# A recommendation tower on one core: the linear layer's output turned to features on partitions, its root taken one step later

## The chip, the cores and the metric

One Trainium2 chip, one of its cores. The metric is the device time of the whole program in microseconds (us), median of the runs shown. Times inside the program come from one profiled execution.

## What is computed

For 512 samples, 26 embedding rows of 64 numbers each are fetched by index, passed through a linear layer and two layer norms, mixed from 26 to 32 rows, and joined with one row made of the dense features. All pairwise inner products of the 33 rows of a sample go through a linear layer (528 to 512) with a layer norm, of which 384 outputs are used, and then through three top layers. Cut to what matters (float32 throughout):

```python
e = stack([tbl_f[ids[:, f]] for f in range(26)], axis=1)      # 512 x 26 x 64
x = layer_norm(dense_t @ Wd.T, gd, bd)                        # 512 x 128
y = layer_norm(einsum('bnd,ed->bne', e, Ws), gs, bs)          # 512 x 26 x 128
y = layer_norm(einsum('bne,pn->bep', y, Wsi), gsi, bsi)       # 512 x 128 x 32
T = concatenate([x[:, None, :], swapaxes(y, 1, 2)], axis=1)   # 512 x 33 x 128
Z = einsum('bnd,bmd->bnm', T, T)                              # 512 x 33 x 33
z = layer_norm(Z[:, TRIL_I, TRIL_J] @ Wl.T, gl, bl)[:, :384]
h = concatenate([z, dense_t], axis=1)
h = maximum(h @ W_top1 + b_top1, 0)                           # 512 wide
h = maximum(h @ W_top2 + b_top2, 0)                           # 256 wide
y = h @ W_top3                                                # 512 x 1
```

## The kernel before

The 512 samples are 4 blocks of 128; a block is 4 units of 32 samples, so there are 16 units and 16 steps `t` (0 to 15), and step `t` works mainly on unit `t`. All engines are programmed by hand, each with its own `step(t)`, and meet only through semaphores; within an engine the order of the text is the order of the work.

- GpSimd (POOL) does one thing for most of the run: 104 indirect gathers (line 239), two for each of the 52 slots of 128 embedding rows. A block has 13 slots; its four units need 4, 3, 3 and 3 new ones. Nothing holds the gathers back.
- In step `t` TensorE (PE) runs `mix(t)` (line 281), which waits for the gathered rows of unit `t` to be scaled (`scale_a`, line 712), then `transposes(t+1)` (line 255), which waits for the gathers of unit `t+1`, then `project(t)` (line 293), `norms(t+1)` (line 266) and `inner(t-1)` (line 305), the inner products of the unit before.
- ScalarE (ACT) runs `keep_u(t)` (line 528), which brings the mixed rows from PSUM and is what `project(t)` waits for, `rows_out(t+1)` (line 515), two `squares_b` (line 534), small roots (`deviation_a`, `deviation_b`), and four `keep_z(t-1, 0..3)` (line 562), which bring the inner products from PSUM and write them across samples into `Zs`.
- VectorE (DVE) runs `add_b` twice (line 719), `mult_a`, `sums_a`, `recip_a` and `scale_a` for unit `t+1`, and `sums_b`, `recip_b` and `norm_b` (line 737) for unit `t`.
- When a block's products are kept, seven small transfers (`relay`, line 196) lay them out on partitions in `Zt`. For the last block the first half goes two units early; the second half is sent after the last product is kept, split over the queues of SP (three), ACT (two) and POOL (two).
- The linear layer and the top layers of block `b` run inside later steps, by `b, j = (t - 6) // 4, (t - 6) % 4`. In step j = 0 PE does the first two of five products of `linear` (line 323), in j = 1 the other three and `layer2` of block b-1, in j = 2 `turn` and a quarter of `layer1`, in j = 3 the rest of `layer1` and `output(b-1)`.
- In `linear` samples are on partitions and the 512 features are the moving side (5 matmuls of 512 columns). So the layer norm works along a row: `stat_w` and `norm_w` on VectorE with one root on ScalarE (a number per partition). The normed values are then turned by PE (`turn`, line 335) and copied back by ScalarE (`keep_zT`, line 574), for which `layer1` (line 347) waits. `layer1` starts from a matmul that puts the dense part `hd` into PSUM (line 340), and `relu1` adds the bias in four instructions (line 583).
- After step 15 the tail runs `inner(15)`, `turn` and `layer1` of block 2, then `last_block`: the dense part, `linear(3)` on all of its transfers, `layer2(2)`, three turns, `layer1` feature by feature, `layer2`, `output`, and a last copy (line 777).

```python
mm = pe.matmul(psW[:, :], Zt[0:KL, b, jj, :], wl_g[0:KL, jj, :], start=(jj == 0),
               stop=(jj == CW - 1))
```

## Time and profile before

| what | value |
|---|---|
| median of 3 runs | 186.33 us (184.78 to 186.76) |
| the profiled execution, whole | 185.44 us |
| its span, first to last instruction | 183.6 us |
| busy PE / DVE / ACT / POOL | 143.7 / 127.4 / 99.6 / 105.7 us |
| mean granted clock of TensorE | 0.972 |

The span lies 1.84 us below the execution's own time. Times in the rows are us from the start of the span. Engines work side by side, so busy times don't add up; a float32 matmul shows as two records in the trace, so that "x10" below is five matmuls.

### The profile page before, as it was taken

What the parts mean: (1) busy time and instruction counts of PE and PEld (TensorE: products, weight loads), DVE (VectorE), ACT (ScalarE), POOL (GpSimd) and SP (SyncE); (2) the same over time, 40 slices, a digit from 0 to 9 for tenths busy, and PEclk for the clock granted to TensorE, in tenths of its full rate; (3) what the DMA queues carried; (4) which work ended last, traced back from release to release, by engine and by line L of the source; (5) the groups of instructions that cost most, each with busy time, mean ns of one, the idle gap of its engine ahead of it and who ended that gap; (6) DMA issues with size and microseconds to landing.
All of it is one profiled execution on the core that took longest, in us unless ns stands there. A gap on an engine that the chain in (4) does not pass through costs nothing.

```text
span 183.6 us, 4383 instructions
## 1 busy us (share of the span) xinstructions
PE 143.7 (78%) x1693; PEld 96.5 (53%) x1693; DVE 127.4 (69%) x297; ACT 99.6 (54%) x233; POOL 105.7 (58%) x111
## 2 busy tenths in 40 slices
PE   0089877899984854899984989699859998869995
PEld 0084444525954433466652675467447654646583
DVE  6099659695989588486989497686957797730321
ACT  3003335582867585556858387755675885812130
POOL 0778777777778778778777777777773000040000
PEclk9999999999998799659999999999999999999999
DMA  4912716141111113111111221111113001020000
GB/s 135 290 49 31 300 22 199 29 118 46 34 27 26 25 25 89 38 29 28 27 26 24 66 65 26 29 31 22 28 40 77 0 5 32 12 34 3 0 0 0
DMA packets 6891, 9.58 MB, mean 52 GB/s; under 512 B 3923, under 2 KB 4056, under 8 KB 6743
## 3 DMA queue, kind: packets, MB, share of 16 engines
q0 software_dynamic: 3504, 3.46, 10.1%
q1 hardware_dynamic: 2845, 5.08, 8.5%
q10 hardware_dynamic: 522, 0.77, 1.7%
q8 instruction: 13, 0.21, 0.4%
q14 instruction: 7, 0.06, 0.1%
HBM read 8.01 MB, written 0.00 MB: 44 GB/s over the span
## 4 chain that ended last, share of the span: by engine, by line
POOL 46%; PE 24%; issue 17%; ACT 5%; DVE 4%; DMA 4%; ACTq 0%; DVEq 0%
POOL g_sb L239 46%; PE psW L323 5%; PE psW L347 3%; PE psH L361 3%; PE psB L293 2%; DMA ids_sb<-in_ids 2%; PE psU L281 2%; PE psZ L305 2%; ACT Zs L562 2%; DMA g_sb<-in_table,row_id 1%; DVE B L719 1%; PE psG L266 1%; ACT U L528 1%; PE psB L388 1%; DVE qA L697 1%
## 5 line engine op out<-in xcount | busy, mean ns | idle before, releaser
L239 POOL DMA_INDIRECT g_sb<-in_table,row_id x104 | 103.1, 991 | 31.7 <-issue 31.4
L562 ACT ACTIVATE Zs<-psZ 32x264 f32<-32x264 f32 x62 | 38.0, 613 | 1.1
L719 DVE TENSOR_TENSOR B<-psB,bias 128x512 f32<-128x512 f32 x32 | 20.6, 685 | 24.2 <-PE psB L293 24.2
L534 ACT ACTIVATE sqB<-B 128x512 f32<-128x512 f32 x32 | 19.7, 632 | 22.0 <-DVE B L719 20.5
L281 PE MATMUL psU<-wsi_x,g_sb 128*128 128x192 f32 (+4 forms) x128 | 22.0, 316 | 10.4 <-DVE g_sb L712 8.0
L281 PEld LDWEIGHTS psU<-wsi_x,g_sb 128*128 128x128 f32 x128 | 19.7, 194 | 16.3 <-DVE g_sb L712 12.6
L737 DVE TENSOR_TENSOR T<-B,rB 128x512 f32<-128x512 f32 x32 | 22.2, 693 | 1.1
L293 PE MATMUL psB<-U,ws_g 64*128 64x512 f32 x64 | 19.6, 692 | 3.7 <-ACT U L528 3.7
L726 DVE TENSOR_REDUCE ssB<-sqB 128x16 f32<-128x512 f32 x32 | 21.6, 678 | 0.1
L266 PEld LDWEIGHTS psG<-gram,sT 128*128 128x128 f32 x104 | 13.4, 198 | 13.4 <-ACT sT L515 10.8
L323 PE MATMUL psW<-wl_g,Zt 127*128 127x512 f32 x40 | 19.5, 621 | 0.4 <-ACT h1T L583 0.4
L266 PE MATMUL psG<-gram,sT 128*128 128x128 f32 x104 | 16.6, 300 | 0.7 <-ACT sT L515 0.7
L255 PE MATMUL psT<-small_sb,g_sb 128*128 128x128 f32 x52 | 11.4, 299 | 4.6 <-DMA g_sb<-in_table,row_id 4.3
L196 POOL DMA_DIRECT2D Zt<-Zs x2 | 2.3, 1137 | 21.9 <-DVE Zs L906 21.9
L528 ACT ACTIVATE U<-psU 128x512 f32<-128x512 f32 x16 | 9.5, 596 | 9.1 <-PE psU L281 8.9
L305 PE MATMUL psZ<-T 128*32 128x33 f32 x1024 | 14.2, 201 | 0.0
L305 PEld LDWEIGHTS psZ<-T 128*32 128x32 f32 x1024 | 12.0, 112 | 3.1 <-issue 1.0
L347 PE MATMUL psW<-zT,w_g 128*128 128x128 f32 x72 | 9.4, 282 | 5.4 <-ACT zT L574 5.4
L347 PEld LDWEIGHTS psW<-zT,w_g 128*128 128x128 f32 x72 | 8.4, 191 | 7.9 <-ACT zT L574 7.8
L323 PEld LDWEIGHTS psW<-wl_g,Zt 127*128 127x128 f32 x40 | 7.2, 195 | 7.3 <-issue 7.1
L515 ACT ACTIVATE sT<-psT 128x384 f32<-128x384 f32 (+1 forms) x16 | 8.2, 515 | 4.7 <-PE psT L255 4.7
L255 PEld LDWEIGHTS psT<-small_sb,g_sb 128*128 128x128 f32 x52 | 6.9, 153 | 7.3 <-DMA g_sb<-in_table,row_id 7.3
(128 smaller groups left out, 184.8 us busy)
## 6 DMA issues: line engine op xcount, KB each, us to landing
g_sb<-in_table,row_id POOLq DMA_INDIRECT x104, 2.5
wl_sb<-in_wl SPq DMA_DIRECT2D x1, 1280.0 KB, 5.5
w_sb<-in_w SPq DMA_DIRECT2D x2, 512.0 KB, 5.7
w_sb<-in_w SPq DMA_DIRECT2D x1, 768.0 KB, 4.3
small_sb<-in_small SPq DMA_DIRECT2D x1, 615.5 KB, 7.0
dense_sb<-in_dense ACTq DMA_DIRECT2D x1, 512.0 KB, 3.7
Zt<-Zs SPq DMA_DIRECT2D x3, 80.0 KB
Zt<-Zs SPq DMA_DIRECT2D x3, 70.0 KB
```

The source lines that it names most:

```text
L239: pool.indirect_dma_start(g_sb[:, k, h * DSP:(h + 1) * DSP], None, table, bass.IndirectOffsetOnAxis(row_id[:, 2 * k + h:2 * k + h + 1], 0) ...
L266: mm = pe.matmul(psG[:, n * P:(n + 1) * P], sT[:, u % 2, n * P:(n + 1) * P], gram[:, :], start=True, stop=True)
L281: mm = pe.matmul(psU[:, (lo - US * j) * PROJ:(hi - US * j) * PROJ], g_sb[:, SLOTS * b + c, :], wsi_x[:, c, lo - s0:hi - s0, :], start=(n = ...
L293: pe.matmul(psB[h][:, :], ws_g[h * DSP:(h + 1) * DSP, :], U[h * DSP:(h + 1) * DSP, u % 2, :], start=True, stop=True).then_inc(B_done, 1)
L305: mm = pe.matmul(psZ[gq * PROJ:(gq + 1) * PROJ, n * COLS:(n + 1) * COLS], T[:, u % 2, h, s, 2:2 + PROJ], T[:, u % 2, h, s, 0:COLS], start= ...
L323: mm = pe.matmul(psW[:, :], Zt[0:KL, b, jj, :], wl_g[0:KL, jj, :], start=(jj == 0), stop=(jj == CW - 1))
L347: mm = pe.matmul(psW[:, f * BS:(f + 1) * BS], w1_g[:, k, f * P:(f + 1) * P], zT[:, k * BS:(k + 1) * BS], start=False, stop=(k == KZ - 1), ...
L534: act.activation(sqB[:, h, :], B[:, h, :], ACT.Square).then_inc(B_squared, 1)
L562: act.activation(to, product, ACT.Copy).then_inc(Z_kept, 1)
L719: dve.tensor_tensor(B[:, h, :].rearrange("p (s j) -> p s j", j=PROJ), psB[h][:, :].rearrange("p (s j) -> p s j", j=PROJ), bias[:, :].rearr ...
L726: dve.tensor_reduce(ssB[:, h, :], sqB[:, h, :].rearrange("p (s j) -> p s j", j=PROJ), AX, ALU.add).then_inc(B_summed, 1)
L737: dve.tensor_tensor(T[:, u % 2, h, :, 2:], B[:, h, :].rearrange("p (s j) -> p s j", j=PROJ), rB[:, h, :].rearrange("p (s o) -> p s o", o=1 ...
```

## The change

The linear layer changes sides. The weights are now stationary in pieces of 128 features and the samples are the moving side: 20 matmuls of 128 columns instead of 5 of 512, with the 512 features of a block's 128 samples on partitions. 12 of the 20 run in step j = 0, the other 8 in j = 1, now ahead of `inner`. `Zs` and `Zt` hold the samples in two halves of 64.

The mean of the layer norm is taken off the weights beforehand: VectorE sums `wl` over features (t = 1) and subtracts it where it scales the weights (now t = 2), and the shift of the extra rows gets its mean off too (t = 2, and an activation in ScalarE's step 3, formerly step 2). The variance is made by squaring the 512 features on ScalarE (`squares_w`) and summing over partitions with a matrix of ones on PE (`variance`, four matmuls of 128 columns), both in j = 1. The root (`deviation_w`, now 128x128) stands at the head of ScalarE's j = 2, the reciprocal (`recip_w`, now 128x128) at the head of VectorE's. The un-normed features go straight from PSUM to `zT` (VectorE, end of j = 1), `layer1` uses them without a turn, whole in j = 2, and its result is scaled by the reciprocal and added to the dense part by VectorE at the head of j = 3 (`scale_h1`, `add_hd`, 128x512 each), then `relu1` is one instruction. `turn`, `keep_zT` on ScalarE, `stat_w`, `norm_w` and the matmul with `hd` are gone. `layer2(b)` runs in j = 3; `relu2`, `output` and `copy_y` of block b come at the head of the next j = 0. The bias is added to `hd` once, in four activations in ScalarE's steps 4 to 7; scaling `w1` moves from VectorE to ScalarE (three activations, t = 2).

In the tail the last unit's products go to another PSUM bank, so `inner(15)` waits for no eviction; `variance(2)` and `layer1(2)` follow; the last block's linear layer is put out in two PSUM banks; `layer2(2)` stands after `layer1(3)`, and `output(2)` just ahead of the last output.

The diff, cut to its core (eight columns of indentation removed):

```diff
+Zs = sb("Zs", [PROJ, 2, 2, 7 * CW, PS])
+Zt = sb("Zt", [P, BLOCKS, 2, CW, PS])
+zT = sb("zT", [P, KZ * BS])
+z_sq = sb("z_sq", [P, FLIN // P * BS])
...
+zr = sb("zr", [P, BS])
...
+psL, psV, psF, psO = [psZ, psT], psU, psB, [psG, psT]
+psS = [psH, psH, psG]
...
+    b, lo = u // BU, 2 * US * (u % 2) + GQ * gq
+    bank = psZ if u < UNITS - 1 else psU
+    return (Zs[:, b % 2, u % BU // 2, 0:COLS, lo:lo + GQ].rearrange("p c s -> p s c"),
+            bank[gq * PROJ:(gq + 1) * PROJ, 0:GQ * COLS].rearrange("p (s c) -> p s c", s=GQ))
...
+    queue.dma_start(Zt[BASE[q]:BASE[q] + ROWS[q], b, lo:hi, :, :],
+                    Zs[FIRST[q] - 1:PROJ, b % 2, lo:hi, CW * q:CW * (q + 1), :]).then_inc(landed, 16)
...
+        if u == UNITS - 1:
+            pe.wait_ge(U_ready, UNITS)
+        elif u:
             pe.wait_ge(Z_kept, 4 * u)
+        bank = psZ if u < UNITS - 1 else psU
...
-                    mm = pe.matmul(psZ[gq * PROJ:(gq + 1) * PROJ, n * COLS:(n + 1) * COLS],
+                    mm = pe.matmul(bank[gq * PROJ:(gq + 1) * PROJ, n * COLS:(n + 1) * COLS],
...
+            pe.wait_ge(d_zt[b], 7 * 16)
+            if b:
+                pe.wait_ge(y_copied, b)
...
-        for jj in range(lo, hi):
-            mm = pe.matmul(psW[:, :], Zt[0:KL, b, jj, :], wl_g[0:KL, jj, :], start=(jj == 0),
-                           stop=(jj == CW - 1))
-        if hi == CW:
+        for n in range(lo, hi):
+            f, jj = n // CW, n % CW
+            mm = pe.matmul(psW[:, f * BS:(f + 1) * BS], wl_g[0:KL, jj, f * P:(f + 1) * P],
+                           Zt[0:KL, b, :, jj, :], start=(jj == 0), stop=(jj == CW - 1))
...
+    def variance(b):
+        pe.wait_ge(W_squared, b + 1)
+        if b == 0:
+            pe.wait_ge(bz_ready, 1)
+        elif b < LAST - 1:
+            pe.wait_ge(h1_scaled, b)
         else:
-            pe.wait_ge(bz_ready, 1)
+            pe.wait_ge(A_mul, UNITS)
+        for f in range(FLIN // P):
+            mm = pe.matmul(psS[b][:, 0:BS], ones_sb[:, :], z_sq[:, f * BS:(f + 1) * BS], start=(f == 0),
+                           stop=(f == FLIN // P - 1))
+        mm.then_inc(W_summed, 1)
+
+    def top1(b, f, to):
         for k in range(KZ):
-            mm = pe.transpose(psH[:, k * P:(k + 1) * P], zn[:, k * P:(k + 1) * P], eye_sb)
-        mm.then_inc(z_tr, 1)
...
+    def layer1(b):
+        pe.wait_ge(zT_ready, b + 1)
+        if b < LAST - 1:
+            pe.wait_ge(W_sd, b + 1)
+        else:
+            pe.wait_ge(h1_scaled, b)
+        if b == 0:
+            pe.wait_ge(w1_ready, 1)
+        for f in range(K1):
+            mm = top1(b, f, psH[:, f * BS:(f + 1) * BS])
+        mm.then_inc(h1_done, 1)
...
     def last_block():
+        pe.wait_ge(d_zt[LAST], 10 * 16)
+        pe.wait_ge(d_zt_act, 2 * 16)
...
+        for f in range(FLIN // P):
+            for jj in range(CW):
+                mm = pe.matmul(psL[f // 2][:, f % 2 * BS:(f % 2 + 1) * BS], wl_g[0:KL, jj, f * P:(f + 1) * P],
+                               Zt[0:KL, LAST, :, jj, :], start=(jj == 0), stop=(jj == CW - 1))
+            if f % 2:
+                mm.then_inc(W_f[f // 2], 1)
...
+        sums_of_squares(0)
+        pe.wait_ge(zT_f[0], 1)
+        pe.wait_ge(zT_f[1], 1)
         pe.wait_ge(B_added, 2 * UNITS)
-        for f in range(K1):
-            pe.matmul(psF[f][:, 0:BS], eye_sb, hd[:, f, LAST * BS:], start=True, stop=False)
-        linear(LAST, 0, CW)
+        top1(LAST, 0, psF[0][:, 0:BS])
+        sums_of_squares(1).then_inc(W_summed, 1)
+        top1(LAST, 1, psF[0][:, BS:2 * BS]).then_inc(h1_f[0], 1)
+        top1(LAST, 2, psF[1][:, 0:BS])
+        top1(LAST, 3, psF[1][:, BS:2 * BS]).then_inc(h1_f[1], 1)
         layer2(LAST - 1)
...
+        pe.wait_ge(W_sd, LAST)
         for k in range(K1):
-            pe.wait_ge(h1T_f[k], 1)
+            if k % 2 == 0:
+                pe.wait_ge(h1T_f[k // 2], 1)
...
+        output(LAST - 1)
...
+        if late and j == 0 and b:
+            output(b - 1)
         project(t)
         if t + 1 < UNITS:
             norms(t + 1)
+        if late and j == 1:
+            linear(b, EARLY, ALL)
...
-            linear(b, 0, 2)
-        if late and j == 1:
-            linear(b, 2, CW)
-            if b:
-                layer2(b - 1)
+            linear(b, 0, EARLY)
+        if late and j == 1 and t < UNITS - 1:
+            variance(b)
         if late and j == 2:
-            turn(b)
-            layer1(b, 0, 1)
+            layer1(b)
         if late and j == 3:
-            layer1(b, 1, K1)
-            if b:
-                output(b - 1)
+            layer2(b)
...
-    output(LAST - 2)
-    turn(LAST - 1)
-    layer1(LAST - 1, 0, K1)
+    variance(LAST - 1)
+    layer1(LAST - 1)
...
+    def squares_w(b):
+        act.wait_ge(W_done, b + 1)
+        if b:
+            act.wait_ge(W_summed, b)
+        act.activation(z_sq[:, :], psW[:, :], ACT.Square).then_inc(W_squared, 1)
...
-        act.wait_ge(W_mv, b + 1)
...
+        bank = psS[b] if b < LAST else psV
+        act.activation(zsd[:, :], bank[:, 0:BS], ACT.Sqrt, bias=eps_c[:, :], scale=1.0 / FLIN).then_inc(W_sd, 1)
...
+        act.wait_ge(h1_added, b + 1)
...
+        act.activation(h1T[:, :], h1[:, :], ACT.Relu).then_inc(h1_ready, 1)
...
+        if late and j == 0 and b:
+            relu2(b - 1)
+        if late and j == 2:
+            deviation_w(b)
...
-        if late and j == 0 and b:
-            relu1(b - 1)
-        if late and j == 2:
-            deviation_w(b)
-            if b:
-                relu2(b - 1)
+        if t == 3:
+            act.wait_ge(m_shift, 1)
+            act.wait_ge(wl_scaled, 1)
+            act.activation(wl_g[0:NA, 0, :], psW[0:NA, :], ACT.Identity, bias=m_off[0:NA, :],
+                           scale=g_i[0:NA, :]).then_inc(m_kept, 1)
+        if late and j == 3:
+            relu1(b)
...
-        if t:
+        if late and j == 1 and t < UNITS - 1:
+            squares_w(b)
+        if 0 < t < UNITS - 1:
             keep_z(t - 1, 0)
         deviation_b(t, 0)
         if t:
+            if t == UNITS - 1:
+                keep_z(t - 1, 0)
+                deviation_b(t, 1)
+                squares_w(b)
             keep_z(t - 1, 1)
             keep_z(t - 1, 2)
-        if late and j == 2:
-            keep_zT(b)
-        deviation_b(t, 1)
+        if t < UNITS - 1:
+            deviation_b(t, 1)
         if t:
             keep_z(t - 1, 3)
...
+            act.wait_ge(d_w1, 16)
+            for k in range(KZ):
+                last = act.activation(w1_g[:, k, :], w1_sb[:, k, :], ACT.Copy, scale=gl_c[:, k:k + 1])
+            last.then_inc(w1_ready, 1)
...
+            act.activation(hd[:, f, :], hd[:, f, :], ACT.Identity, bias=b1_z[:, f:f + 1]).then_inc(hd_biased, 1)
...
+        relay(act, LAST, q, 1, 2, d_zt_act)
+    deviation_w(LAST - 1)
     relu1(LAST - 1)
+    for g in range(2):
+        act.wait_ge(W_f[g], 1)
+        act.wait_ge(zT_f[g], 1)
+        act.activation(z_sq[:, 2 * g * BS:2 * (g + 1) * BS], psL[g][:, 0:2 * BS], ACT.Square).then_inc(sq_f[g], 1)
     deviation_w(LAST)
...
+    def keep_zT(b):
+        dve.wait_ge(W_squared, b + 1)
         if b:
...
+            dve.wait_ge(h1_done, b)
+        dve.tensor_copy(zT[:, :], psW[:, 0:FOUT]).then_inc(zT_ready, 1)
...
+    def recip_w(b):
         dve.wait_ge(W_sd, b + 1)
+        if b:
+            dve.wait_ge(h1_scaled, b)
         dve.reciprocal(zr[:, :], zsd[:, :]).then_inc(W_recip, 1)
+
+    def scale_h1(b):
         dve.wait_ge(W_recip, b + 1)
+        dve.wait_ge(h1_done, b + 1)
...
-            dve.wait_ge(z_tr, b)
...
+            dve.wait_ge(h1_ready, b)
+        dve.tensor_tensor(h1[:, :].rearrange("p (f s) -> p f s", f=K1),
+                          psH[:, :].rearrange("p (f s) -> p f s", f=K1),
+                          zr[:, :].rearrange("p (o s) -> p o s", o=1).broadcast_to([P, K1, BS]),
+                          ALU.mult).then_inc(h1_scaled, 1)
...
+    def add_hd(b):
+        dve.wait_ge(h1_scaled, b + 1)
...
+        h = h1[:, :].rearrange("p (f s) -> p f s", f=K1)
+        dve.tensor_tensor(h, h, hd[:, :, b * BS:(b + 1) * BS], ALU.add).then_inc(h1_added, 1)
...
+        for g, n in ((0, 2 * BS), (1, BS)):
+            dve.wait_ge(W_f[g], 1)
+            dve.tensor_copy(zT[:, 2 * g * BS:2 * g * BS + n], psL[g][:, 0:n]).then_inc(zT_f[g], 1)
+        recip_w(LAST)
...
+        for g in range(2):
+            h = h1[:, 2 * g * BS:2 * (g + 1) * BS].rearrange("p (f s) -> p f s", f=2)
+            dve.wait_ge(h1_f[g], 1)
+            dve.tensor_tensor(h, psF[g][:, 0:2 * BS].rearrange("p (f s) -> p f s", f=2),
+                              zr[:, :].rearrange("p (o s) -> p o s", o=1).broadcast_to([P, 2, BS]),
+                              ALU.mult).then_inc(h1s_f[g], 1)
+            dve.wait_ge(h1s_f[g], 1)
+            dve.tensor_tensor(h, h, hd[:, 2 * g:2 * (g + 1), LAST * BS:], ALU.add).then_inc(h1a_f[g], 1)
...
         if late and j == 2:
-            stat_w(b)
-            norm_w(b)
+            recip_w(b)
+        if late and j == 3:
+            scale_h1(b)
+            add_hd(b)
+        if t == 2:
+            dve.wait_ge(m_done, 1)
+            dve.bn_stats(mstat[0:NA, :], psW[0:NA, :]).then_inc(m_prep, 1)
+            dve.wait_ge(m_prep, 1)
+            dve.bn_aggr(mmv[0:NA, :], mstat[0:NA, :]).then_inc(m_prep, 1)
+            dve.wait_ge(m_prep, 2)
+            dve.tensor_scalar(m_off[0:NA, :], mmv[0:NA, 0:1], -1.0, g_i[0:NA, :], ALU.mult,
+                              ALU.mult).then_inc(m_shift, 1)
...
+        if late and j == 0 and b:
+            copy_y(b - 1)
...
+        if late and j == 1:
+            keep_zT(b)
         if t == 1:
             dve.wait_ge(d_wl, 16)
+            dve.tensor_reduce(wl_sum[:, :], wl_sb[:, :, :], AX, ALU.add).then_inc(wl_summed, 1)
+            dve.wait_ge(wl_summed, 1)
+            dve.tensor_scalar(wl_mean[:, :], wl_sum[:, :], 1.0 / FLIN, None, ALU.mult).then_inc(wl_summed, 1)
+        if t == 2:
+            dve.wait_ge(wl_summed, 2)
             for jj in range(CW):
-                last = dve.tensor_scalar(wl_g[:, jj, :], wl_sb[:, jj, :], gg[:, jj:jj + 1], None, ALU.mult)
+                last = dve.tensor_scalar(wl_g[:, jj, :], wl_sb[:, jj, :], wl_mean[:, jj:jj + 1],
+                                         gg[:, jj:jj + 1], ALU.subtract, ALU.mult)
             last.then_inc(wl_scaled, 1)
...
-    stat_w(LAST - 1)
...
+    recip_w(LAST - 1)
+    scale_h1(LAST - 1)
+    add_hd(LAST - 1)
```

## Rows read from the trace of the kernel before

**Rows 1.** The page's chain that ended last, shares by engine.
```profile
POOL 46%; PE 24%; issue 17%; ACT 5%; DVE 4%; DMA 4%; ACTq 0%; DVEq 0%
```
**Rows 2.** The chain in order of time: start, length, what; where POOL leaves it.
```profile
115.84 2.50 DMA g_sb<-in_table,row_id
...
118.39 0.33 PE psT L255
```
**Rows 3.** Timeline of POOL (start, length, engine, line): its last gather.
```profile
138.77 0.94 POOL L239 DMA_INDIRECT g_sb<-in_table,row_id  x1 [0.30 <-issue]
```
**Rows 4.** Timeline of PE and ACT in steps 8, 11 and 12; idle time in brackets.
```profile
100.40 0.94 PE L347 MATMUL psW<-zT,w_g 128*128 128x128 f32 x6 [2.74 <-ACT zT L574]
...
122.65 0.30 ACT L522 ACTIVATE sdA<-qA,eps_c 128x8 f32<-128x8 f32 x1 [0.74 <-DVE qA L700]
...
134.41 0.49 ACT L574 ACTIVATE zT<-psH 128x384 f32<-128x384 f32 x1
...
134.96 0.94 PE L347 MATMUL psW<-zT,w_g 128*128 128x128 f32 x6 [2.62 <-ACT zT L574]
```
**Rows 5.** Timeline of step 14, a step with little beside its own work.
```profile
144.40 0.60 ACT L528 ACTIVATE U<-psU 128x512 f32<-128x512 f32 x1
...
145.05 1.13 PE L293 MATMUL psB<-U,ws_g 64*128 64x512 f32 x4 [0.36 <-ACT U L528]
...
146.21 1.29 DVE L719 TENSOR_TENSOR B<-psB,bias 128x512 f32<-128x512 f32 x2 [1.01 <-PE psB L293]
...
149.47 0.56 DVE L712 TENSOR_TENSOR g_sb<-g_sb,rA 128x384 f32<-128x384 f32 x1
...
151.06 0.62 ACT L562 ACTIVATE Zs<-psZ 32x264 f32<-32x264 f32 x1
...
151.70 0.60 ACT L528 ACTIVATE U<-psU 128x512 f32<-128x512 f32 x1
151.71 0.69 DVE L737 TENSOR_TENSOR T<-B,rB 128x512 f32<-128x512 f32 x1
```
**Rows 6.** Groups by shape, whole span: count, busy us, mean ns of one.
```profile
L562 ACT ACTIVATE Zs<-psZ 32x264 f32<-32x264 f32 x62 | 38.0, 613 | 1.1
...
L534 ACT ACTIVATE sqB<-B 128x512 f32<-128x512 f32 x32 | 19.7, 632 | 22.0 <-DVE B L719 20.5 <-issue 1.5
...
L323 PE MATMUL psW<-wl_g,Zt 127*128 127x512 f32 x40 | 19.5, 621 | 0.4 <-ACT h1T L583 0.4
...
L347 PE MATMUL psW<-zT,w_g 128*128 128x128 f32 x72 | 9.4, 282 | 5.4 <-ACT zT L574 5.4
...
L731 DVE RECIPROCAL rB<-sdB 128x16 f32<-128x16 f32 x32 | 7.8, 245 | 0.8 <-ACT sdB L540 0.8
...
L705 DVE RECIPROCAL rA<-sdA 128x8 f32<-128x8 f32 x4 | 0.8, 194 | 0.4 <-ACT sdA L522 0.4
```
**Rows 7.** Timeline of the tail.
```profile
159.81 1.22 DVE L906 COPY Zs<-psZ 32x264 f32<-32x264 f32 x2 [0.46 <-PE psZ L305]
...
163.59 2.94 PE L347 MATMUL psW<-zT,w_g 128*128 128x128 f32 x24
...
167.85 4.53 PE L323 MATMUL psW<-wl_g,Zt 127*128 127x512 f32 x10 [0.43 <-ACT h1T L583]
...
181.75 0.28 DVE L777 COPY y_sb<-psZ 1x128 f32<-1x128 f32 x1 [0.54 <-PE psZ L402]
```
**Rows 8.** The transfers' issues: POOL's two (ns min/median/max, starts); the later one's landing.
```profile
L196 POOL DMA_DIRECT2D Zt<-Zs x2: 636/1137/1638, 161.6 to 163.2; - x2
...
Zt<-Zs POOLq DMA_DIRECT2D x1, 3.8 KB, 3.5
```
**Rows 9.** A PE start after idling, then stretches: busy us of each engine (records), PE's granted clock.
```profile
73.46 1.36 PE L281 MATMUL psU<-wsi_x,g_sb 128*128 128x96 f32 x8 [2.33 <-issue]
...
58.00:61.00 3.00, 3.00 (x12) 2.21 (x12) 1.77 (x5) 2.13 (x5) 2.39 (x3) 0.52 0.11 22
...
76.00:82.00 6.00, 6.00 (x76) 3.54 (x77) 3.13 (x6) 2.34 (x6) 4.48 (x5) 0.50 0.15 30
```

216 lines of the change are left out of this document (71 added, 145 removed).

## The prediction, made before the changed kernel was run

> **What bounds the kernel now.** I read the chain of waits first. By shares POOL carries 46% of it and PE 24% [rows 1]; in order of time the chain is POOL's gathers, one after the other, until 118.39, where PE can turn the first rows of the last block, and from there it runs through PE, ScalarE and VectorE to the end [rows 2]. So there are two regimes. Before 118.39 compute only has to be on time for the gathers, and what it saves there is lost. After it 63 us of compute are left (to the last copy at 181.75 [rows 7]), and each us saved there counts, as long as no later gather gates it: the last is issued at 138.77 [rows 3].
>
> Then the timelines. Step 14 is a plain step [rows 5]: `keep_u` at 144.40, `project` at 145.05, `add_b` at 146.21, `scale_a` done at 150.03, the last eviction done at 151.68, the next `keep_u` at 151.70, the last `norm_b` done at 152.40. So a step takes 7.30 us, and its three loops close within a few tenths: VectorE's (`add_b` + 3.82, then `mix`), ScalarE's (`add_b` + 5.47, and `keep_u` stands right behind the last eviction with no idle time), and PE's. What is put into ScalarE between `squares_b` and the next `keep_u` lengthens the step by its own time. Steps 8 and 12 have one more thing: PE stands 2.74 and 2.62 us for `keep_zT`, which stands behind evictions on ScalarE [rows 4].
>
> In the tail the last product is kept at 161.03, `linear(3)` starts at 167.85, and the last copy stands at 181.75 [rows 7].
>
> **The change part by part.** Prices first. A record of 128 columns costs 2.94/24 = 0.12 us in a row of them, one of 512 costs 4.53/10 = 0.45 [rows 7]. So 20 narrow matmuls (40 records, about 4.5 us) cost what 5 wide ones did. `variance` (8 records, 0.9) takes the place of three turns and the wide matmul with `hd` (1.3): PE's sum per block stays.
>
> The Trainium skill speaks against the narrow form (TensorE: Matmul & The Clock Gate, "Back-to-back issue gap"): in a stream of weight loads and matmuls it gives 81 ns per matmul of 128 columns and 131 ns per one of 512, so four narrow ones would cost 2.5 times a wide one. This trace differs: 4 x 0.12 against 0.45. I go by the trace; the rule's case is a rival below.
>
> A wide `squares_w` is priced as the 128x512 square, 0.63 [rows 6]. The 128x128 root isn't in the trace: at least 0.30 (128x8 [rows 4]), at most 0.63 (128x512); I take 0.35. The 128x128 reciprocal isn't either: 8 elements cost 194 ns, 16 cost 245 [rows 6], so 6.4 ns each and 0.245 + 112 x 0.0064 = 0.96 us; bounds 0.28 (a 128-element copy [rows 7]) and 1.3 (a slope a third steeper). `scale_h1` and `add_hd` cost half of `add_b`'s pair each, 0.65 [rows 5]. An eviction now writes samples at steps of 256 bytes in place of 512. It costs 0.61 for 264 elements where 512 contiguous ones cost 0.60 (`keep_u` [rows 5]), so the stride costs something; halving it gives between -0.2 (no such cost left) and +0.2 (twice that cost) each. I take 0: either way each element goes to a place far from the last.
>
> *Before 118.39.* Added to ScalarE: three activations of 0.63 for one in step 2 (`project(3)` about 1 us late), 0.65 for `hd` at the end of each of steps 4 to 7, squares and root in step 7. I find `keep_u(8)` about 2.2 us late. Then step 8 loses its stall of 2.74 [rows 4] and is level again; in step 10 `relu2` at the head delays `keep_u` by 0.6, and `transposes(12)` is ready at about 118, just ahead of the gather. VectorE's new sums (2560 elements, about 2.8 us in place of 2.1) lie under PE's work in step 1. I take 0 for all this; it is tight, and up to 1 us late lies in the range.
>
> *Steps 11 to 14*, forward from `project(11)` at 118.65, with the intervals of step 14:
> Step 11: `add_b` 119.81 as before. PE: norms to 120.9, 8 of linear to 122.6, inner to 123.4. ScalarE: `deviation_a` done 122.95 [rows 4], squares to 123.55, so variance to 124.5 and `mix(12)` behind it. Four evictions and two roots (3.05) to 126.6, `deviation_w` to 126.95, `keep_u(12)`; `project(12)` 127.6. VectorE: `keep_zT` and the reciprocal are done at 128.5, ahead of `add_b(12)` at 128.75.
> Step 12: scaled at 132.6, but `layer1` holds PE to 133.1 (project, norms, inner, 24 records); `mix(13)` ends 134.2, evictions end 134.2, `keep_u(13)` 134.35. No wait for `zT`.
> Step 13: `norm_b(12)` done 134.95, then 1.3 to 1.4 of `scale_h1` and `add_hd`: `add_b(13)` 136.4 where 136.15 was possible. Evictions end 141.9, `relu2` 0.6, `keep_u(14)` 142.45, against 144.40 [rows 5]. The last gather, issued 138.77 and landing 2.5 later as the one in [rows 2], 141.3, is just in time.
> Step 14: PE has 12 of linear (2.7) for 2.0; `mix(15)` 148.5, evictions end 149.7, `keep_u(15)` 149.95, against 151.70: 1.75 us gained in four steps. Of the stall of 2.62 about a third is given back to ScalarE's chain.
>
> *To the last block.* In step 15 ScalarE is never idle from its first square, at `add_b(15)` 151.76 + 0.72: two squares 1.23, x 0.25, two roots 0.58, six evictions 3.68, `squares_w` 0.60, together 6.34: all products kept at 158.8, against 161.03. `layer2` no longer stands before `inner(15)`, and the other bank frees it from evictions. The transfers: POOL's first issue took 1.64 us with five pieces a row and its second, with few rows, 0.64 [rows 8]; with one piece a row both take 0.64, so the second goes at 160.0. It landed 3.5 us after its start [rows 8]; a gather takes 2.5 [rows 2]. So 162.5 to 163.5; I take 163.3 for the start of `linear(3)`. PE has done `layer1(2)` by 160.4; the relu of block 2, with 0.96 + 1.3 on VectorE ahead of it, is done by 164.2, under `linear(3)`. Before, it stood in front of it: `layer1(2)` and the relus, not the transfers (landed 163.2 + 3.5 = 166.7), set 167.85. Now the transfers do. Gain here 167.85 - 163.3 = 4.55, with the 1.75 in it.
>
> *Last block*, along PE: linear 4.5, sums of squares 0.45, `layer1` by four 2.65 with the second sums 0.45 in it, `layer2(2)` 1.8, `layer2(3)` 1.8, outputs 0.5 and 0.6, and 0.2 of waits: 12.9, against 181.75 - 167.85 = 13.9. Beside it the root (about +6.2), reciprocal 0.96, two scalings and two additions of about 0.45 and the relu end at +9.8, as `layer2(2)` ends at +9.8: nothing to spare, so a dearer reciprocal shows at once. Gain 1.0.
>
> *Sum*: 4.55 + 1.0 = 5.55; less 0.2 for handovers not listed, 5.35. From the profiled execution's 185.44 (span 183.6 and 1.84 around it) that is 180.1, and as the median lies 0.89 above that execution, **181.0 us**.
>
> **The rivals.**
> A, the clock falls in the wait for the transfers. PE would idle from 160.4 to 163.3, longer than anywhere late in the trace. After idling 2.33 us at 73.46, PE was at 0.50 (1.2 GHz) from 76 to 82; another low stretch was 58 to 61 [rows 9]. Against it: after 2.74 and 2.62 us [rows 4] it stayed high. Half speed for 3 us costs 1.5, for 6 us up to 3: 182.5 to 184. The Trainium skill (TensorE: Matmul & The Clock Gate, "HAM oscillation") says that waits for DMA send the engine back to the low clock; this trace does it only at times.
>
> B, the steps gain nothing: compute reaches the gate at 118.39 up to 1 us late, or ScalarE's chain takes back all of the stall. Then 1.75 to 2.75 go: 182.8 to 183.8. For it: no loop of a step has over 0.3 us to spare.
>
> C, slower: the evictions get dearer. Four stand in ScalarE's loop in each step, so x us each add 4x a step, and as compute is barely on time from step 4 on, about 12 steps add up: 48x. At x = 0.2 that is 9.6 and the time 190.6; it decides from x = 5.35/48 = 0.11. For it: the stride has a visible price and changes. Against: the element count and the distance class don't.
>
> D, narrow matmuls don't run at the pace of [rows 7] with this operand (two runs of 64 samples), but at their own duration, 0.28 [rows 6]: `linear(3)` 11.3 in place of 4.5, steps 14 and 15 longer by some 3: 190.8.
>
> E, evictions or transfers are cheaper (x = -0.2 saves some 0.5 beside VectorE's loop in four steps, landing at 162.5 saves 0.8): 179.
>
> **How the numbers follow.** Forecast 0.45, A 0.22, B 0.17, C 0.07, D 0.03, E 0.06. A measurement of this kernel tells about 1% (1.9 us) from no change. Faster by over 1% is below 184.5: all of the forecast, A but for a tail, most of B, E: 0.81. A and B together, or a mild C, give no change: 0.11. C and D slower: 0.08. The range 178.5 to 185.0 holds E to A and B; the forecast's own is 179.5 to 182.
>
> **What would show it.** In the new profile: no wait of PE for `zT` in steps 8 and 12; `project(12)` near 127.6 and `keep_u(15)` near 150; products kept near 158.8 and `linear(3)` near 163.3, ended by the transfers; reciprocals of 128x128 near 0.96; evictions at 0.61; last copy near 176.4. It is wrong if `keep_u(15)` comes at 151.7 as before, if evictions change by over 0.1 us, or if the granted clock is low after 160.

## The result, and the profile after the change

The changed kernel takes 178.23 us, the median of 5 runs (177.62 to 181.22). The kernel before took 185.70 beside it (5 runs). The ratio is 0.958, with a 95% interval from 0.953 to 0.963; two of the five executions, of 181.22 and 181.14 us, lie over 1.5% above the fastest and are not in it. I had forecast 181.0 with a range from 178.5 to 185.0, so the direction was right, the size was 2.8 us short, and the time fell just below the range.

The profiled execution is one of 181.22 us with low stretches of the granted clock in the first 75 us, so it reaches the gate about 3 us late. (The gate is the place in step 11 where TensorE turns the first rows of the last block and then starts `project(11)`: 118.65 before, 121.73 here.) For this reason I compare stretches between two instructions rather than times of day.

The chain that ended last, shares by engine, of the changed kernel:

```profile
PE 39%; ACT 16%; DVE 15%; issue 12%; POOL 11%; DMA 5%; SPq 1%; ACTq 0%; DVEq 0%
```

POOL had 46% of it [rows 1] and has 11%: in this execution compute was late, and the gathers set little.

Timeline of TensorE (start, length, engine, line; in brackets the idle time before it and what ended it), from `project(11)` to the last block:

```profile
121.73 1.13 PE L307 MATMUL psB<-U,ws_g 64*128 64x512 f32 x4 [0.25 <-ACT U L557]
...
130.11 1.13 PE L307 MATMUL psB<-U,ws_g 64*128 64x512 f32 x4 [0.95 <-ACT U L557]
...
132.73 2.94 PE L358 MATMUL psH<-zT,w_g 128*128 128x128 f32 x24
...
160.10 2.84 PE L358 MATMUL psH<-zT,w_g 128*128 128x128 f32 x24
164.43 2.50 PE L399 MATMUL psZ<-Zt,wl_g 127*128 127x128 f32 x20 [1.49 <-DMA Zt<-Zs]
```

The row at 132.73 is `layer1` in step 12. It has no bracket: the wait for `zT` is gone (2.62 in [rows 4]). In step 8 `layer1` starts at 101.48, without a wait too. In the last row the transfers end TensorE's wait, as forecast, but it is only 1.49 us long. Between them `project` goes from step 11 to step 12 in 8.38 us (130.11 - 121.73).

Timeline of ScalarE at the end of step 11, and `keep_u` of steps 11 and 15:

```profile
121.08 0.60 ACT L557 ACTIVATE U<-psU 128x512 f32<-128x512 f32 x1 [0.28 <-PE psU L295]
...
126.47 0.63 ACT L591 ACTIVATE Zs<-psZ 32x264 f32<-32x264 f32 x1
126.90 0.26 ACT L569 ACTIVATE sdB<-ssB,eps_c 128x16 f32<-128x16 f32 x1
127.19 1.28 ACT L591 ACTIVATE Zs<-psZ 32x264 f32<-32x264 f32 x2
128.27 0.26 ACT L569 ACTIVATE sdB<-ssB,eps_c 128x16 f32<-128x16 f32 x1
128.55 0.63 ACT L591 ACTIVATE Zs<-psZ 32x264 f32<-32x264 f32 x1
129.21 0.37 ACT L604 ACTIVATE zsd<-psH,eps_c 128x128 f32<-128x128 f32 x1
129.47 0.59 ACT L557 ACTIVATE U<-psU 128x512 f32<-128x512 f32 x1
...
152.16 0.60 ACT L557 ACTIVATE U<-psU 128x512 f32<-128x512 f32 x1
```

Each start is to be held against the start and length before it. The root at 129.21 lasts 0.37, and yet `keep_u` starts 0.26 later. An eviction of 0.63 is followed after 0.43 (126.47 to 126.90). Lengths overlap there (not behind the small roots of 128x16, whose 0.26 is followed after 0.29 and 0.28), and a sum of lengths is too long. `keep_u(11)` to `keep_u(15)` takes 31.08 us.

ScalarE's last two evictions, with which all products are kept (159.74 + 1.26 = 161.0):

```profile
159.74 1.26 ACT L591 ACTIVATE Zs<-psU 32x264 f32<-32x264 f32 x2
```

VectorE's last copy, and then POOL's two transfers (ns min/median/max and starts of the issues; the landings of the large one and of the small one):

```profile
177.53 0.28 DVE L830 COPY y_sb<-psH 1x128 f32<-1x128 f32 x1 [0.16 <-PE psH L433]
```
```profile
L210 POOL DMA_DIRECT2D Zt<-Zs x2: 535/549/563, 161.3 to 161.8; - x2
...
Zt<-Zs POOLq DMA_DIRECT2D x1, 28.8 KB, 1.9
...
Zt<-Zs POOLq DMA_DIRECT2D x1, 3.8 KB, 2.0
```

These answer [rows 8]. An issue takes 0.55 where they took 1.64 and 0.64, and the later one lands after 2.0 us where it took 3.5.

But POOL's are no longer the last. The chain that ended last, in order of time (start, length, what), goes from the last kept product through SP's three issues:

```profile
161.03 0.55 SPq L210
...
161.62 0.77 SPq L210
...
162.44 1.95 DMA Zt<-Zs
```

POOL's second transfer starts at 161.8 and lands at 163.8, SP's third starts at 162.44 and lands at 164.39, and `linear(3)` starts at 164.43.

Groups by shape (count, busy us, mean ns of one, idle time before them):

```profile
L591 ACT ACTIVATE Zs<-psZ 32x264 f32<-32x264 f32 x60 | 37.0, 618 | 1.5 <-PE psZ L322 0.4
...
L791 DVE RECIPROCAL zr<-zsd 128x128 f32<-128x128 f32 x4 | 3.8, 951 | 4.8 <-ACT zsd L604 4.7
...
L597 ACT ACTIVATE z_sq<-psW 128x512 f32<-128x512 f32 x3 | 1.7, 576 | 0.0
...
L604 ACT ACTIVATE zsd<-psH,eps_c 128x128 f32<-128x128 f32 x2 | 0.7, 368 | 0.1
```

The eviction is unchanged (613 before [rows 6]), and the reciprocal takes 0.951 where 0.96 was forecast.

Stretches of the same execution (busy us and records of PE, PEld, DVE, ACT and POOL, then PE's granted clock, DMA share, GB/s):

```profile
33.00:40.00 7.00, 6.57 (x77) 3.06 (x77) 4.05 (x9) 2.99 (x9) 5.17 (x7) 0.52 0.21 38
...
57.00:75.00 18.00, 13.79 (x172) 10.08 (x170) 12.38 (x26) 11.48 (x26) 13.73 (x15) 0.62 0.18 35
...
164.00:172.00 8.00, 7.57 (x65) 7.43 (x66) 2.93 (x6) 1.77 (x4) 0.00 (x0) 1.00 0.01 2
```

The low level (1.2 GHz) shows early; behind the wait for the transfers the clock stays at its upper level.

In stretches, in us:

| stretch | before | forecast | after |
|---|---|---|---|
| `project(11)` to `project(15)` | 33.70 | 31.95 | 31.08 |
| `project(15)` to products kept | 8.7 | 8.2 | 8.2 |
| products kept to `linear(3)` (161.0 to 164.43 after) | 6.8 | 4.5 | 3.4 |
| `linear(3)` to the last copy | 13.9 | 13.1 | 13.1 |
| `project(11)` to the last copy | 63.1 | 57.75 | 55.8 |

### The profile page after: what moved, and what is told of

Read it like the earlier page. It is cut to its first block, busy times and chain, and to the rows that moved or that the text cites. A ratio compares the mean times of both kernels' runs of the same rounds, so it can differ in the third digit from the quotient of the medians.

```text
span 179.4 us, 4637 instructions
## 1 busy us (share of the span) xinstructions
PE 144.5 (81%) x1819; PEld 110.4 (62%) x1819; DVE 134.3 (75%) x299; ACT 102.3 (57%) x230; POOL 104.1 (58%) x111
## 3 DMA queue, kind: packets, MB, share of 16 engines
q0 software_dynamic: 3392, 3.45, 10.0%
## 4 chain that ended last, share of the span: by engine, by line
PE 39%; ACT 16%; DVE 15%; issue 12%; POOL 11%; DMA 5%; SPq 1%; ACTq 0%; DVEq 0%
POOL g_sb L253 11%; PE psB L307 9%; ACT Zs L591 8%; PE psW L338 5%; PE psU L295 5%; PE psG L280 4%; DVE B L759 4%; PE psZ L322 4%; ACT U L557 3%; DVE qA L737 3%; DVE prod L730 3%; DMA ids_sb<-in_ids 3%; PE psW L461 2%; ACT sdB L569 2%; DVE ssB L766 2%
## 5 line engine op out<-in xcount | busy, mean ns | idle before, releaser
L295 PE MATMUL psU<-wsi_x,g_sb 128*128 128x192 f32 (+4 forms) x128 | 23.3, 330 | 9.6 <-DVE g_sb L752 9.6
L295 PEld LDWEIGHTS psU<-wsi_x,g_sb 128*128 128x128 f32 x128 | 21.0, 207 | 12.8 <-DVE g_sb L752 12.0
L338 PE MATMUL psW<-Zt,wl_g 127*128 127x128 f32 x120 | 14.8, 278 | 0.0
L338 PEld LDWEIGHTS psW<-Zt,wl_g 127*128 127x128 f32 x120 | 13.9, 192 | 0.9 <-issue 0.8
L210 POOL DMA_DIRECT2D Zt<-Zs x2 | 1.1, 549 | 21.4 <-ACT Zs L591 21.4
L307 PEld LDWEIGHTS psB<-U,ws_g 64*128 64x128 f32 x64 | 5.4, 207 | 11.9 <-ACT U L557 11.6
L269 PE MATMUL psT<-small_sb,g_sb 128*128 128x128 f32 x52 | 10.1, 298 | 1.8 <-DMA g_sb<-in_table,row_id 1.5
L730 DVE TENSOR_TENSOR prod<-psG,g_sb 128x384 f32<-128x384 f32 (+1 forms) x16 | 9.3, 584 | 2.1 <-PE psG L280 2.1
L551 ACT ACTIVATE sdA<-qA,eps_c 128x6 f32<-128x6 f32 (+1 forms) x16 | 4.8, 301 | 9.7 <-DVE qA L740 9.7
L752 DVE TENSOR_TENSOR g_sb<-g_sb,rA 128x384 f32<-128x384 f32 (+1 forms) x16 | 9.5, 592 | 0.6
```

The lines of the kernel that those rows point to most:

```text
L295: mm = pe.matmul(psU[:, (lo - US * j) * PROJ:(hi - US * j) * PROJ], g_sb[:, SLOTS * b + c, :], wsi_x[:, c, lo - s0:hi - s0, :], start=(n = ...
L307: pe.matmul(psB[h][:, :], ws_g[h * DSP:(h + 1) * DSP, :], U[h * DSP:(h + 1) * DSP, u % 2, :], start=True, stop=True).then_inc(B_done, 1)
L338: mm = pe.matmul(psW[:, f * BS:(f + 1) * BS], wl_g[0:KL, jj, f * P:(f + 1) * P], Zt[0:KL, b, :, jj, :], start=(jj == 0), stop=(jj == CW - 1))
```

## The experiments

**The changed kernel repeated.** No edit.

> The changed kernel again, for a profile of an undisturbed execution. The profile in hand (181.2 us) has TensorE at its low clock from 34 to 40 us and reaches project(11) at 121.7, 3.3 us behind the gate that the gathers set at 118.4. Theory: the four steps behind the gate and the tail are the same in every execution (55.8 us from project(11) to the last copy) and only the arrival differs, so a 177.7 us execution has project(11) at 118.2 to 119 and the last copy 55.8 us later. Rival: the steps behind project(11) differ too; then this interval is not 55.8 within 0.3.

Median 178.03 us, ratio to the kernel before 0.960 (0.954 to 0.966). Its profiled execution, 180.4 us, is again one that comes late to the gate (`keep_u(11)` at 120.28, the clock at 0.67 from 52 to 76) and again takes 31.06 from there to `keep_u(15)` and 25.37 on to the last copy. What was gained from step 11 on repeats to 0.1 us. An execution of 178 us was not profiled, so the other half of the expectation, where such a one passes the gate, stays open.

**The old layout of `Zs` and `Zt`.** One part of the change undone: samples in one row of 128 again, so that a transfer's pieces are 256 bytes.

```diff
-Zs = sb("Zs", [PROJ, 2, 2, 7 * CW, PS])
-Zt = sb("Zt", [P, BLOCKS, 2, CW, PS])
+Zs = sb("Zs", [PROJ, 2, 7 * CW, BS])
+Zt = sb("Zt", [P, BLOCKS, CW, BS])
...
-queue.dma_start(Zt[BASE[q]:BASE[q] + ROWS[q], b, lo:hi, :, :],
-                Zs[FIRST[q] - 1:PROJ, b % 2, lo:hi, CW * q:CW * (q + 1), :])
+queue.dma_start(Zt[BASE[q]:BASE[q] + ROWS[q], b, :, lo * PS:hi * PS],
+                Zs[FIRST[q] - 1:PROJ, b % 2, CW * q:CW * (q + 1), lo * PS:hi * PS])
```

> The change with only the layout of the products' two buffers put back (samples in one run of 128, so that the last half block goes in five pieces of 256 bytes a row and not one of 1280). Theory: fewer pieces made the last transfers land sooner, 3.4 us from the last kept product to linear(3) in place of the 5.65 worked out for before; putting the layout back costs 2.2 us (ratio to the changed kernel 1.012). Evictions stay at 0.61 to 0.62 us (the stride of their writes, 512 or 256 bytes, doesn't matter). Rival 1: the pieces cost nothing and the start moved for the order of the tail alone: no difference within 0.3 us. Rival 2: the stride matters: evictions differ by over 0.03 us.

Median 183.88, ratio 0.989 (0.981 to 0.997): 5.9 us of the gain are gone. TensorE's timeline and one stretch:

```profile
157.97 2.84 PE L358 MATMUL psH<-zT,w_g 128*128 128x128 f32 x24
165.03 4.61 PE L399 MATMUL psZ<-Zt,wl_g 127*128 127x128 f32 x20 [4.22 <-DMA Zt<-Zs]
169.43 2.77 PE L399 MATMUL psT<-Zt,wl_g 127*128 127x128 f32 x20
```
```profile
163.00:170.00 7.00, 4.97 (x23) 5.00 (x24) 1.09 (x3) 0.63 (x1) 0.00 (x0) 0.53 0.07 6
```

Two things are lost. The wait grows from 1.49 to 4.22 us (POOL's landings are 4.5 and 3.7), so that kept to `linear(3)` takes 6.06 in place of 3.4. And then the clock falls: half of the layer takes 4.61 in place of 2.50, and `linear(3)` to the last copy 15.54 in place of 13.1. I had expected the first alone. The two make 5.1 of the 5.9; steps 11 to 14 are 0.4 longer here (31.48), with a wait of 0.58 for a gather among them. The strided evictions take 619 ns here and 618 with the new layout: halving the stride changed nothing there.

**The old layout with the wait filled.** The same, with 18 products of 128 columns, which nothing reads, in the wait.

```diff
+pe.wait_ge(B_added, 2 * UNITS)
+for _ in range(18):
+    pe.matmul(psB[0][:, 0:P], eye_sb, eye_sb, start=True, stop=True)
 last_block()
```

> The old layout of the last layer with its idle time filled by products. In two runs on slow chips linear layer 3's first half took 2.47 us behind the filling (4.61 without it). If the fall of the clock cost the second half of the old layout's loss, the ratio to the kernel before is 0.973 (0.968 to 0.979), about 181 us here. Rival: the loss stays whole, ratio 0.989.

Median 182.11, ratio 0.976 (0.969 to 0.983), inside the forecast. The interval of the run without the filling, 0.981 to 0.997, overlaps it slightly, so the timeline has to carry the reading:

```profile
161.25 4.18 PE L393 MATMUL psB<-small_sb 128*128 128x128 f32 x36
165.79 2.47 PE L403 MATMUL psZ<-Zt,wl_g 127*128 127x128 f32 x20 [0.35 <-DMA Zt<-Zs]
168.10 2.40 PE L403 MATMUL psT<-Zt,wl_g 127*128 127x128 f32 x20
```

The transfers land no sooner, but the layer runs at 2.47 and 2.40, and `linear(3)` to the last copy takes 13.07 again. So the fall of the clock came from TensorE's idleness and costs 2.4 us behind a wait of 4.2. With that shown, the layout's worth at this place is 2.6 for the landing and 2.4 for the clock.

**`layer2(2)` ahead of `linear(3)`, as before.**

```diff
 def last_block():
+    layer2(LAST - 1)
     pe.wait_ge(d_zt[LAST], 10 * 16)
...
     top1(LAST, 3, psF[1][:, BS:2 * BS]).then_inc(h1_f[1], 1)
-    layer2(LAST - 1)
```

> The change with layer2 of block 2 put back in front of the last block's linear layer. Theory: the relu of block 2 ends 166.3 in the profile in hand, two us after linear(3) starts there; in front of it linear(3) starts at 168.1 in place of 164.4, and the 1.8 us of layer2 are saved behind it: 1.9 us slower than the changed kernel. Rival: PE idles for the transfers there anyway, so that layer2 is hidden in the wait: no difference.

Median 183.91, ratio 0.990 (0.982 to 0.997). Timeline, and a stretch:

```profile
163.17 3.78 PE L380 MATMUL psW<-h1T,w_sb 128*128 128x128 f32 x16 [3.45 <-ACT h1T L610]
166.74 3.62 PE L400 MATMUL psZ<-Zt,wl_g 127*128 127x128 f32 x20
```
```profile
160.00:167.00 7.00, 3.83 (x18) 3.83 (x19) 2.34 (x3) 0.64 (x2) 0.00 (x0) 0.68 0.03 6
```

Kept to the last copy is 22.5 us, where the changed kernel takes 16.5. The 6.0 are three things, of which I had priced the first. TensorE idles 3.45 us for the relu, and by the order alone `linear(3)` starts 3.7 late, as expected. The clock is low behind that wait: `layer2` takes 3.78 in place of 1.95 and the first half of `linear(3)` 3.62 in place of 2.50, by their starts 2.9 us together. And `layer2`, gone from behind `layer1`, saves 0.7 there and not its 1.8, since TensorE now stands 0.89 us for the last block's relu.

**Block 1's copy of `zT` back on ScalarE in step 12**, behind two evictions, where it stood before.

```diff
 keep_z(t - 1, 1)
 keep_z(t - 1, 2)
+if late and j == 2 and b == 1:
+    act.activation(zT[:, :], psW[:, 0:FOUT], ACT.Copy).then_inc(zT_ready, 1)
```

Expected, after two runs on chips where every kernel took some 300 us (told below):

> The changed kernel with block 1's copy of the summary products on ScalarE behind two evictions of step 12. In two runs on slow chips, keep_u of step 12 to keep_u of step 13 took 12.6 and 12.8 us against 7.32: TensorE stood 3.77 idle and layer 1 behind it took 4.38 instead of 2.94. If that holds where the kernel before takes some 186 us, that step takes 12.6 here and the median lies 5.3 above the changed kernel's: 183.4 (182.4 to 184.6). Rival: the gathers bound keep_u of step 15 anyway and hide a part: 181.5.

Median 183.50, ratio 0.988 (0.982 to 0.994). Timeline of TensorE, and a stretch:

```profile
129.32 0.77 PE L322 MATMUL psZ<-T 128*32 128x33 f32 x64
133.86 4.57 PE L358 MATMUL psH<-zT,w_g 128*128 128x128 f32 x24 [3.78 <-ACT zT L595]
```
```profile
133.00:139.00 6.00, 5.14 (x30) 5.14 (x31) 2.24 (x5) 1.61 (x4) 4.47 (x6) 0.72 0.23 50
```

One copy of 0.49 us, moved to another engine, is worth 5.3: a wait of 3.78, and `layer1` at 4.57 in place of 2.94 behind it. `keep_u(12)` to `keep_u(13)` takes 12.79 in place of 7.33. `layer1` now follows `inner` directly in step 12, so the old place costs more here than the 2.62 it cost before [rows 4], after which the clock had stayed up.

Each of these three parts, put back alone, costs 5.3 to 5.9 us, 17 together, where the whole change gained 7.5. So they are not shares of the gain: each makes or lengthens an idle time in the new order, and the low clock behind it comes on top. The narrow products and the other bank for `inner(15)` were not put back by themselves.

**The early scalings on VectorE.** The scaling of `w1` and the four additions to `hd` go from ScalarE's steps 2 and 4 to 7 to VectorE's steps 3 and 4 to 7.

```diff
-act.activation(w1_g[:, k, :], w1_sb[:, k, :], ACT.Copy, scale=gl_c[:, k:k + 1])
+dve.tensor_scalar(w1_g[:, k, :], w1_sb[:, k, :], gl_c[:, k:k + 1], None, ALU.mult)
...
-act.activation(hd[:, f, :], hd[:, f, :], ACT.Identity, bias=b1_z[:, f:f + 1])
+dve.tensor_scalar(hd[:, f, :], hd[:, f, :], b1_z[:, f:f + 1], None, ALU.add)
```

> The change with the early scalings taken off ScalarE: the three of w1 on VectorE at the end of step 3, the four additions of the bias to the dense part on VectorE at the end of steps 4 to 7. Theory: on ScalarE they stand in front of the next keep_u and make compute miss the gate at 118.4; off it, project(11) is at 118.7 and the time falls by what e1 is late, 0.3 to 1 us. Rival: the lateness comes from TensorE's low clock in the early steps alone: no difference within 0.3 us. Second rival: VectorE has no room at the end of these steps and add_b gets late: slower by 0.5 or more.

Median 178.95 (176.62 to 180.52), ratio 0.959 (0.948 to 0.970), beside 0.960 for the changed kernel on the same chip: no gain that the scatter lets one see, and a median 0.9 higher. `keep_u(9)` came at 100.1 (105.52 in the profile of after, 101.73 in the earliest one with the same steps and no filling, layer 2 first), but TensorE then stood at the gathers of the next units:

```profile
108.44 0.33 PE L269 MATMUL psT<-small_sb,g_sb 128*128 128x128 f32 x1 [1.11 <-DMA g_sb<-in_table,row_id]
109.52 0.33 PE L269 MATMUL psT<-small_sb,g_sb 128*128 128x128 f32 x1 [0.75 <-DMA g_sb<-in_table,row_id]
```

and `keep_u(11)` came at 118.45 (`project(11)` at 119.11, where 118.7 was expected). Behind these waits the granted clock was 0.79 from 112 to 118.

**Filling TensorE early.** Eight products that nothing reads (some 1.8 us) at the end of TensorE's steps 3, 4 and 5, where the clock had been low.

```diff
+if 3 <= t <= 5:
+    if t == 3:
+        pe.wait_ge(bz_ready, 1)
+    for _ in range(8):
+        pe.matmul(psH[:, 0:P], eye_sb, eye_sb, start=True, stop=True)
 if late and j == 0:
     linear(b, 0, EARLY)
```

> The early filling, where the kernel before takes about 185 us: the gate's keep_u of step 11 at 118.4 or less, no execution above 179, median 177.8 (177.0 to 178.2). Rival 1: the clock is not held, the executions stay mixed, 178 to 181. Rival 2: the filling delays each mix, 179.5 to 182.

Median 178.37 (177.07 to 178.92), ratio 0.957 (0.947 to 0.967). No execution is above 179, as expected, and the median lies 0.2 above the range expected. The clock is held (0.990 over the span, 0.943 in the profile of after), and `keep_u(11)` is at 115.85, 5.2 us ahead of the profile of after. But the median is that of the changed kernel. TensorE's timeline, and then POOL's last gather, show where the lead goes:

```profile
117.84 0.33 PE L269 MATMUL psT<-small_sb,g_sb 128*128 128x128 f32 x1 [1.70 <-DMA g_sb<-in_table,row_id]
...
125.98 0.33 PE L269 MATMUL psT<-small_sb,g_sb 128*128 128x128 f32 x1 [0.56 <-DMA g_sb<-in_table,row_id]
133.72 0.33 PE L269 MATMUL psT<-small_sb,g_sb 128*128 128x128 f32 x1 [0.44 <-DMA g_sb<-in_table,row_id]
...
141.48 0.33 PE L269 MATMUL psT<-small_sb,g_sb 128*128 128x128 f32 x1 [0.68 <-DMA g_sb<-in_table,row_id]
```
```profile
139.01 0.95 POOL L253 DMA_INDIRECT g_sb<-in_table,row_id  x1 [0.30 <-issue]
```

and its chain that ended last:

```profile
POOL 58%; issue 18%; PE 14%; DMA 5%; ACT 3%; SPq 1%; DVE 0%; ACTq 0%
```

Every step from 11 to 14 waits for its gathers. The last is issued at 139.01 and reaches TensorE at 141.48, and `keep_u(15)` stands at 149.01. The gate is no longer at the first rows of the last block, but at its last.

**Both together.**

> The early filling with the early scalings on VectorE. Where no gather held them, steps 4 to 8 were 0.44 us shorter each than with the scalings on ScalarE. If the gathers bound the gate, it is at 117.3 to 118.5 here and the median 176.6 to 178.0. Rival: the gate comes at 115 or below, median 174 to 175.5.

Four executions: 176.82, 176.84, 180.58 and 180.74, median 178.71, above the 176.6 to 178.0 expected. The profiled one (176.84) has `keep_u(11)` at 116.31, between the forecast (117.3 to 118.5) and the rival (115 or below), so that neither held, and `keep_u(15)` at 147.78. POOL's last gather there:

```profile
137.89 0.94 POOL L253 DMA_INDIRECT g_sb<-in_table,row_id  x1 [0.30 <-issue]
```

It is issued 1.12 us sooner than in the run before, and TensorE waits for it there too (0.54, until 140.25): `keep_u(15)` comes 1.23 sooner because the gathers do, and not by the scalings. Whether this kernel is faster stays open: two of its four executions are below every one of the early filling on the same chip, two are slower than the changed kernel's median. The mean clock does not tell them apart: at 0.971, which the two slower ones had, this study has executions from 176.62 to 181.14. What parts the executions of 177 from those of 181 stays open; with the filling they occur too.

**An inconclusive series, and what could be read from it.** On three chips all kernels, the one before too, took some 300 us (304.2, 304.7 and 303.3 before). In the first two or three steps the engines waited 100 to 120 us more than elsewhere, which no row explains; the gathers ran at their usual pace. One of the three, by its number, where the kernel before took 303.3, took 185.6 for it some 36 minutes later (the chip of the copy on ScalarE and the filled old layout above), so this is no fixed property of a chip. Ten runs fell there: the copy on ScalarE (300.69, repeated 298.54), the filled old layout (297.22, 297.73), the early filling (293.71, 293.31, 293.88), both together (291.14, 290.64) and the root below (295.24). Nine expectations, first those of the first time:

> The changed kernel, with one copy moved: block 1's summary copy from psW to zT in step 12 stands on ScalarE behind two evictions instead of on VectorE. The prediction counted the wait of TensorE in steps 8 and 12 (2.74 and 2.62 us before) as the stall that goes, and the trace of after has none there. If that copy's place is what removed it, TensorE waits 3.0 to 3.6 us in step 12 for the copy, the mix of step 13 comes about 3.4 us later, and the median is 181.0 to 182.0. Rival: ScalarE and TensorE have slack enough in step 12 that the wait is hidden behind other work; then the time is under 1 us above the changed kernel's, 178.0 to 179.2.

> The earlier run with the old layout of the last layer (its 256-byte pieces) took 183.88 us. There the time from the last products kept to the first product of linear layer 3 was 6.06 us, of which TensorE stood 4.22 us idle, and after it the granted clock was 0.50 for some 7 us, with the first half of the layer at 4.61 us instead of 2.50. Here 18 products without use (128 columns each, some 4 us) stand in that idle time, nothing else is changed. If the clock's fall after the idle time is what cost the second half of the loss, the landing stays at about 6.06 us, the clock stays near 1.0 behind it, linear layer 3's start to the last copy is 13.1 us instead of 15.54, and the median is 180.6 (179.8 to 181.6). Rival: the slower first half has another cause (the old layout's products themselves); then the clock is high and the time still 183.9, or the clock falls in spite of the filling and it is 183.9 or more.

> The changed kernel with 8 products without use (some 1.8 us) at the end of TensorE's steps 3, 4 and 5, where the profile of after shows the granted clock low and the gate reached 3 us late. If those executions of 180 to 181 us among ones of 178 come from the clock's fall there, and the filling keeps it up, then the gate's keep_u of step 11 starts at 118.4 or less (121.08 in the profile of after, 120.28 in the repeated one), no execution is above 179, and the median is 177.8 (177.0 to 178.2). Rival 1: the clock is not held by so little work, and the executions stay mixed, median 178 to 181. Rival 2: the filling stands in the way of the mix in those steps and delays each by up to 1.8 us; then the median is 179.5 to 182.

> The kernel of the early filling, with the scalings of steps 3 to 5 on VectorE instead of ScalarE as well. The scalings on VectorE alone brought keep_u of step 9 to 100.1 (105.52 in the profile of after) but the gate at 118.45 all the same, after waits for the gathers of step 10 and a fall of the clock behind them, for 178.95 us. If the gathers bound the gate, it is at 117.3 to 118.5 here too, and the median is 176.6 to 178.0, equal to the early filling alone within 1 us. Rival: with the clock held the gate comes earlier by the gain in steps 3 to 9 as well, 115 or below, and the median is 174 to 175.5.

> The same kernel as the run with block 1's copy on ScalarE, whose executions took some 300 us like those of the kernel before on that chip, since the first two steps stood waiting for 120 us there. In its undisturbed part, keep_u of step 12 to keep_u of step 13 took 12.59 us, against 7.32 in the three kernels beside it: 5.3 us more, not the 3.4 that I had expected. If that holds, the median here is 178.1 + 5.3 = 183.4 us (182.4 to 184.4), and step 12 to 13 takes 12.6. Rival: part of it is hidden where the gathers still run, and it is 181.5.

> The old layout of the last layer with its idle time filled by products. In the run on the other chip the clock stayed up behind the filling: linear layer 3's first half took 2.47 us (4.61 without the filling). If the clock's fall cost the second half of the loss, the median is 180.6 (179.8 to 181.6) here. Rival: 183.9 as without the filling.

> The early filling: the gate's keep_u of step 11 at 118.4 or less, no execution above 179, median 177.8 (177.0 to 178.2). Rival 1: the clock is not held and the executions stay mixed, 178 to 181. Rival 2: the filling delays each mix, 179.5 to 182.

> The early filling and the early scalings on VectorE. In the run on the other chip the steps from 2 to 7 were some 0.5 us shorter each than with the scalings on ScalarE, where no gather held them. If the gathers bound the gate here, it is at 117.3 to 118.5 and the median 176.6 to 178.0. Rival: the gate comes at 115 or below, median 174 to 175.5.

> The early filling once more, if the chip runs the kernel before in about 185 us: the gate's keep_u of step 11 at 118.4 or less, no execution above 179, median 177.8 (177.0 to 178.2). Rival 1: the clock is not held, the executions stay mixed, 178 to 181. Rival 2: the filling delays each mix, 179.5 to 182.

They were made for a kernel before of 185 us, and the totals decide nothing. But the last gather is issued at 137 us or sooner, and by 160 us all have landed, and from then on each step runs as fast as compute allows. `keep_u(11)` to `keep_u(15)` takes 31.01 to 31.04 us there in the seven with these steps unchanged: so 31.08 in the profile of after is compute's own pace. And in the steps where the scalings move, each step is 0.44 us shorter with them on VectorE (7.36 against 7.80): that gain is real, and in the runs of 177 to 181 us the gathers take it.

**The root behind `keep_u` again**, as before the change, on one of those chips.

```diff
-if late and j == 2:
-    deviation_w(b)
 keep_u(t)
 if t + 1 < UNITS:
     rows_out(t + 1)
+if late and j == 2:
+    deviation_w(b)
```

> The changed kernel with the root of step 2 of a block put back behind the keep_u and rows_out of its step, as before the change. By the prediction's terms each root ahead of keep_u costs 0.35 of ScalarE before it and saves VectorE's head wait for it. If the root's early place matters, keep_u of steps 4, 8, 12 comes 0.25 to 0.4 earlier here but the biased sums of the step (queued behind the reciprocal of 0.95) 0.5 to 0.7 later, and the time from keep_u(11) to keep_u(15) is 31.4 (31.04 with the early root), the median 0.3 to 1 above the changed kernel's. Rival: the reciprocal has slack and the early root only delays keep_u: then keep_u(11) to keep_u(15) is 30.7 and the median 0.3 to 1 below.

`keep_u` of steps 11, 12 and 13, here and, in the second fence, in the run beside it with the root at the head:

```profile
235.22 0.60 ACT L557 ACTIVATE U<-psU 128x512 f32<-128x512 f32 x1
243.30 0.60 ACT L557 ACTIVATE U<-psU 128x512 f32<-128x512 f32 x1
250.89 0.60 ACT L557 ACTIVATE U<-psU 128x512 f32<-128x512 f32 x1
```
```profile
232.02 0.60 ACT L565 ACTIVATE U<-psU 128x512 f32<-128x512 f32 x1
240.36 0.59 ACT L565 ACTIVATE U<-psU 128x512 f32<-128x512 f32 x1
247.68 0.60 ACT L565 ACTIVATE U<-psU 128x512 f32<-128x512 f32 x1
```

Step 11 is 0.26 shorter (8.08 against 8.34) and step 12 0.27 longer (7.59 against 7.32); all four take 31.05 against 31.02. Neither expectation held: in this stretch the root's place is worth nothing. (The run beside it has the early filling too, so the medians, 295.24 and 293.88, can't be compared.)

## Why the prediction was right in kind, and where it was wrong

Right in kind, and in these sizes:
- *The stall in steps 8 and 12* is gone, and it was the copy's place that made it: with the copy back on ScalarE it returns (shown in step 12).
- *The prices*: reciprocal 0.951 (0.96), root 0.368 (0.35), squares 0.576 (0.63), evictions unchanged at 0.618, the last linear layer 4.73 us for 40 records (4.5). So C is out (x is 0.005, and it needed 0.11), and D: four narrow matmuls do cost what one wide one does. The estimate of 2.5 times, worked out from two figures of the Trainium skill (TensorE: Matmul & The Clock Gate, "Back-to-back issue gap"), does not hold for this kernel's records: 0.118 us for 128 columns against 0.45 for 512.
- *The last block*, 13.1 us to the last copy, and the transfers as what sets `linear(3)`, though by SP's third and not by POOL's second, as the forecast had it.
- *The arrival at the gate*, 0 net, is not shown and not refuted. The forecast has `project(11)` at 118.65. The two profiles of the changed kernel have it at 121.73 and 120.93, with the low clock ahead of it; four runs with the same steps before the gate have it at 118.02 (layer 2 first), 119.07 (the copy on ScalarE), 119.11 (the old layout) and 120.12 (the same, filled).

Wrong in three terms, which together make the 2.8 us; the step that failed most is the price of the transfers:
- *"It landed 3.5 us after its start"*, carried over (as 3.3, from a span of 2.5 to 3.5) to pieces five times as long. From the last kept product the forecast counts 1.2 us to the last issue, on POOL, and 3.3 to its landing, 4.5 in all; measured are 1.4 to the last issue, on SP, and 1.95 to its landing, 3.4 in all: 1.1 us. The pieces' number was changed by the very edit I was pricing, and I let it shorten POOL's issue but not the landing. A row of the trace pointed there: a gather lands in 2.5 [rows 2]. The Trainium skill (DMA: Bandwidth & Descriptors, "Why small descriptors are slow (HBM only)") says that transfers from SBUF to SBUF don't suffer the penalty of small pieces, and means bandwidth. In latency they do here, by the runs: 4.5 and 3.7 us with the old layout, 1.9 and 2.0 with the new one, at the same bytes.
- *"Four evictions and two roots (3.05) to 126.6, deviation_w to 126.95"*. ScalarE's work was summed by lengths, and starts stand closer: the same stretch is 2.74 long, and the root adds 0.26. The four steps took 31.08 and not 31.95: 0.9 us, 0.57 of it in step 11; the other 0.30, spread over steps 12 to 14, was not traced further. The Trainium skill has this (ScalarE: Activation LUTs, "What ACT_TABLE_LOAD costs"): activations back to back overlap by about 93 ns. The rows agree in kind, with 0.11 behind the root of 128x128, 0.20 behind an eviction and none behind a root of 128x16. An estimate from that page, 8 handovers from the squares to `keep_u(12)`, would have taken 0.7 us off the sum; the rows give 0.47 there (lengths of 3.99, 3.52 by the starts).
- *"as the median lies 0.89 above that execution"*. That was a median of three. With five runs it is 185.70, 0.26 above, and executions of one kernel scatter by more than that. The offset should have widened the range and not moved the forecast: 0.6 to 0.9 us.

1.1, 0.9 and 0.6 to 0.9 are 2.6 to 2.9, against 2.8 seen. The first two are measured; that the sum closes also takes an execution of 178 us to pass the gate as forecast, which was not profiled, so part of the close fit may be luck.

*Rival A* had its mechanism right and its condition unmet. The clock does fall behind waits of this place, when they are 3.45 (layer 2 first) or 4.22 us (old layout); here the wait is 1.49. The rule of the Trainium skill named in the forecast (TensorE: Matmul & The Clock Gate, "HAM oscillation"), that waits for DMA send the engine back to the low clock, is borne out by the old layout; layer 2 first and step 12 show the same fall behind waits for ScalarE. It also means that the new layout pays twice. *Rival E* gave 179 with a landing at 162.5, and was the nearest of the five, by its transfers and not by its evictions.

One thing the forecast said in passing now matters most: the last gather "is just in time". Compute alone, 31.04 us from a `keep_u(11)` at 118.0, reaches `keep_u(15)` at 149.0. The gathers allow it no sooner: with compute 2 us earlier (the early filling) they held it at 149.01. The run with layer 2 first, whose steps are the changed kernel's, had `keep_u(11)` at 117.34, waited for gathers in steps 12, 13 and 14 (0.40, 0.48 and the row below), and had `keep_u(15)` at 148.93:

```profile
141.40 0.33 PE L269 MATMUL psT<-small_sb,g_sb 128*128 128x128 f32 x1 [0.58 <-DMA g_sb<-in_table,row_id]
```

From there the last copy is 25.4 us off in six profiles with the new tail (25.37 to 25.39), and an execution takes 3.7 more: 178.0 to 178.1, which is the median. So the kernel stands at the crossing of both bounds. For its own executions of 177.6 to 178.2 this is argued, since they were not the profiled ones. And the gathers' bound moves: in the ten profiles of kernels at 177 to 186 us the last gather is issued between 137.71 and 139.97.

## What to carry to other kernels

When an edit takes away a wait of TensorE, or makes one, price the granted clock behind it as well: three experiments here lost 1.6, 2.4 and 2.9 us of clock on top of waits of 3.5 to 4.2 us, and in the one where it was tried, filling the wait with useless products got it back. A transfer's landing has to be priced anew when the edit changes the number of its pieces, even between on-chip places, and every queue that issues a part of it has to be followed to its last landing; and a chain on one engine is to be summed from starts and not from lengths. Then look for the next bound: work saved ahead of a fixed stream of gathers ends as waiting for it.

## What the runs showed of the hardware that was not expected

- Pieces of 256 bytes against pieces of five times that, between two places on chip: landing 3.7 to 4.5 against 1.8 to 2.0 us, and the issue on POOL at most 1.64 against at most 0.56, at equal bytes.
- The clock after a wait: at its upper level behind 1.49, 2.62 and 2.74 us, at the lower one behind 3.45, 3.78 and 4.22 us. Early in the run, where TensorE stands often, it was low behind 2.33 us too [rows 9], so the length of one wait does not decide it alone.
- An eviction of 264 elements with a stride in the destination takes 0.61 to 0.62 us at steps of 256 bytes and of 512 alike.
- Three chips ran every kernel tried there in about 300 us, with the same work at the same pace once the first steps were over; one of them ran the kernel before in 185.6 us some 36 minutes later.
- The stream of 104 gathers, which waits for nothing, issues its last one between 137.71 and 139.97 us.
